# Row sums of the head-mixing softmax: added up by VectorE in place of ScalarE's accumulator output

## The reference, cut to what matters

```
scores = jnp.einsum('bshd,bsgd->bshg', q, k) * inv_sqrt_dk   # 16 x 16 per token
attn = jax.nn.softmax(scores, axis=-1)
out = jnp.einsum('bshg,bsgd->bshd', attn, v)
```

## Time and profile before

| | |
|---|---|
| median of three runs | 6372.72 us |
| profiled execution | 6376.72 us, span 6374.9 us |
| TensorE (PE) busy | 5567.3 us, 87% |
| VectorE (DVE) busy | 4532.6 us, 71% |
| ScalarE (ACT) busy | 3991.2 us, 63% |
| GpSimd (POOL) busy | 1513.1 us, 24% |
| mean granted TensorE clock | 0.892 |

### The profile page before, as it was taken

One profiled execution on the slowest core, in us unless ns is written; L12 is line 12 of the kernel. 1 busy time (PEld: TensorE's weight loads), 2 busy tenths in 40 slices (PEclk: granted clock), 3 DMA queues, 4 the chain that ended last, 5 costly groups with the idle time before them and its releaser, 6 DMA issues. The chain is left out here.

```text
span 6374.9 us, 111016 instructions
## 1 busy us (share of the span) xinstructions
PE 5567.3 (87%) x38530; PEld 3816.5 (60%) x38530; DVE 4532.6 (71%) x16189; ACT 3991.2 (63%) x9761; POOL 1513.1 (24%) x2564
## 2 busy tenths in 40 slices
PE   5889889898988989889898988889899898989976
PEld 3566566566656666566566656656556566656643
DVE  1377777677786677786677787767687676786774
ACT  2566666666676666676665676766576665666642
POOL 0122222222222222222222222222222222222221
PEclk7789898999999899898998989989898999988865
DMA  2000000000000000000000000000000000000000
GB/s 83 4 4 8 4 10 6 6 6 6 8 6 10 4 8 6 6 8 6 6 8 5 8 6 10 6 6 6 6 8 6 6 8 5 7 6 8 3 4 6
DMA packets 29382, 53.45 MB, mean 8 GB/s; under 512 B 8145, under 2 KB 9810, under 8 KB 27986
## 3 DMA queue, kind: packets, MB, share of 16 engines
q1 hardware_dynamic: 28770, 45.73, 2.3%
HBM read 37.33 MB, written 8.39 MB: 7 GB/s over the span
## 5 line engine op out<-in xcount | busy, mean ns | idle before, releaser
L997 POOL TENSOR_TENSOR t_pr<-t_pr,sc 128x512 f32<-128x512 f32 x512 | 654.4, 1278 | 1298.2 <-ACT t_pr L921 1296.4
L970 DVE MATCH_REPLACE8 wk<-m,wk 128x256 f32<-128x256 f32 x2048 | 822.9, 410 | 0.0
L966 DVE MAX8 m<-wk 128x8 f32<-128x256 f32 x2048 | 759.6, 413 | 0.0
L407 DVE TENSOR_REDUCE m_nm<-bankM 128x2 f32<-128x512 f32 x1024 | 651.1, 682 | 74.2 <-PE bankM L397 73.2
L732 ACT ACTIVATE xk_area<-bankH,xb 64x256 f32<-64x256 f32 x1024 | 479.8, 469 | 343.9 <-PE bankH L638 325.8
L456 PE MATMUL bankM<-m_q,m_kT 32*128 32x512 f32 x2048 | 652.2, 720 | 0.0
L927 ACT ACTIVATE t_pr<-t_pr,t_nm 128x256 f32<-128x256 f32 x1024 | 463.6, 502 | 196.0 <-POOL t_pr L997 192.3
L397 PE MATMUL bankM<-m_kT,m_q 32*128 32x256 f32 x4096 | 537.5, 389 | 24.8 <-DVE m_nm L407 15.7
L797 DVE TENSOR_REDUCE xnm<-bankH 128x4 f32<-128x512 f32 x256 | 176.1, 688 | 467.6 <-PE bankH L661 467.2
L498 PE MATMUL bankT<-ident,t_pr 128*128 128x128 f32 x2048 | 380.7, 316 | 140.6 <-ACT t_pr L927 139.6
L991 POOL TENSOR_SCALAR mx<-m 128x2 f32<-128x2 f32 x512 | 118.0, 231 | 1584.9 <-DVE wk L970 1579.8
(11 more groups left out here) (208 smaller groups left out, 11837.7 us busy)
## 6 DMA issues: line engine op xcount, KB each, us to landing
xin<-x_in SPq DMA_DIRECT2D x32, 256.0 KB, 3.1
ctxA<-ctx_in SPq DMA_DIRECT2D x32, 256.0 KB, 2.6
ctxB<-ctx_in SPq DMA_DIRECT2D x32, 256.0 KB, 2.8
out<-x SPq DMA_DIRECT2D x32, 256.0 KB, 2.2
w<-w_w SPq DMA_DIRECT2D x2, 1024.0 KB
xwq<-w_xwq SPq DMA_DIRECT2D x1, 1024.0 KB
xwk<-w_xwk SPq DMA_DIRECT2D x1, 1024.0 KB
xwv<-w_xwv SPq DMA_DIRECT2D x1, 1024.0 KB
```

What stands on the lines that cost most here:

```text
L407: nc.vector.tensor_reduce(b["nm"][:, i % 2, 2 * (i // 2) + x, :], banks[u % 4][:].rearrange("p (j s) -> p j s", j=2), AX.X, ALU.max, negat ...
L966: link.inc(nc.vector.max(top, src[:, t, :]))
L970: m = nc.vector.match_replace(out=wk[:, k, t, :], in_to_replace=take, in_values=src[:, t, :], imm_value=-BIG)
L997: nc.gpsimd.tensor_tensor(sp_[:, u % 2], taken[:, u % 2], sc[:, u % 3], ALU.mult).then_inc(g["sp_mul"], 1)
```

## The change

The exponentials lose `accum_out`. VectorE gets one `tensor_reduce` for each quad that adds up the rows of the four tiles in `xp`, and signals a new semaphore `hm_rs`, for which the reciprocal behind it waits. Nothing else of the program differs.

```
@@ COUNTS
-              ... hm_rr=8, hm_s=8, ...
+              ... hm_rr=8, hm_rs=8, hm_s=8, ...
@@ scalar_h
                         nc.scalar.activation(xp[s % 3][:, i, :], bankH[0][:, i * P:(i + 1) * P], ACT.Exp,
-                                             bias=xnm[:, c:c + 1], accum_out=xrs[:, c:c + 1]).then_inc(g["hm_ex"], 1)
+                                             bias=xnm[:, c:c + 1]).then_inc(g["hm_ex"], 1)
@@ vector_h
                     dve.wait_ge(*at(g["hm_ex"], 4 * q + 4))
+                    nc.vector.tensor_reduce(xrs[:, 4 * q:4 * q + 4], xp[q % 3], AX.X, ALU.add).then_inc(g["hm_rs"], 1)
+                    dve.wait_ge(*at(g["hm_rs"], q + 1))
                     nc.vector.reciprocal(xrr[:, 4 * q:4 * q + 4], xrs[:, 4 * q:4 * q + 4]).then_inc(g["hm_rr"], 1)
```

More of the change, by code:

```diff
@@ L101 @@
               crs_qT=2, crs_rd=2, crs_s=16, crs_sp=4, crs_st=16, crs_v=1, crs_va=1, crs_x=1, crs_y=1, ctxA_in=16, ctxB_in=16, dveC=1,
-              dveH=2, dveT=240, hm_ev=48, hm_ex=32, hm_nm=8, hm_o=8, hm_ot=8, hm_pn=8, hm_proj=12, hm_pt=8, hm_rr=8, hm_s=8, hm_tr=8,
+              dveH=2, dveT=240, hm_ev=48, hm_ex=32, hm_nm=8, hm_o=8, hm_ot=8, hm_pn=8, hm_proj=12, hm_pt=8, hm_rr=8, hm_rs=8, hm_s=8, hm_tr=8,
               hm_vev=4, hm_vtr=4, hm_x2=1, hm_xb=1, hm_y=1, latT=1, lat_ps=1, len_in=16, lin_o=1, lin_xb=1, lin_y=1, ln0_rstd=1, ln0_stat=5,
```

## The result

The changed kernel takes 6497.5 us (median of 4 runs) beside 6380.7 us of the kernel before: ratio 1.0182, 95% interval 1.0152 to 1.0211. It is slower, by 116 us where 88 were forecast (6497.5 us where the forecast has 6460). The profiled executions lie 6491.8 and 6376.7 us, 115 us apart, with a mean granted clock of 0.881 and 0.892.

A forecast was written before the change was run, and what follows sets the result against it. VectorE was taken to bound the full stretches, where it never pauses; 89 us there plus 10 in open stretches less 11 from dropped reads gave +88 us, forecast 6460 us, 8-in-10 range 6390 to 6540.

The forecast's parts named there:

- The full stretches, 124 x 0.72 = 89: Where VectorE never pauses, each of 124 quads' reduction and wait adds its full 0.72 us: 89 us.
- in the full stretch TensorE is not what is awaited, so I cost it at nothing: GpSimd normalising 0.72 us later per quad was priced at zero, since TensorE is not awaited in stretches where VectorE never pauses.
- At most 22 us come back from the reads, I take 11: Dropped ScalarE reads gain only in open stretches, where scores wait for exponentials: at most 62 x 4 x 0.09, half taken.
- The open stretches let a tenth through, 10: Where VectorE has idle time, its waits absorb most of 132 x 0.72 = 95 us of additions; 10 us remain.
- the 2 to 3 expected: Sign in the open stretch: VectorE's wait at line 797 should shrink by 2 to 3 us.
- The sum: Whole kernel: 89 + 10 - 11 = +88 us on the profiled 6376.7 us; forecast 6460 us, 1.4% slower.
- The top of the forecast's own range, 6505: Upper end of the forecast's own range, 6420 to 6505, from path terms up to 89 + 30 and a 30 us clock shift.
- TensorE is the true bound, the additions are absorbed: Rival: in the full stretches VectorE's additions fill slack and only the excess counts, about 6385 us; chance 0.17.
- ScalarE's gain decides: Rival: in the open stretch dropped reads outweigh the additions, faster, about 6281 us if all reads count; chance 0.05.
- Every reduction counts: Rival: open-stretch quads delay the next maximum too, so all additions cost, 6373 + 184 - 11 = 6546 us; chance 0.10.
- The reduction is stretched by GpSimd's traffic: Rival: GpSimd's traffic slows VectorE's sum to, say, twice its length, giving 6548 us; chance 0.03.
- If the mean granted clock moves by more than 0.01, part of the difference is the clock's: Sign: a shift of TensorE's mean granted clock above 0.01 means part of the difference is not the order's.

The follow-up runs named there:

- e4: The change for quads 5 to 8 of each sample alone, quads 1 to 4 keeping the accumulator output; 1.0200 of the kernel before, 127 us slower.
- e3: The change for quads 1 to 4 of each sample alone, quads 5 to 8 keeping the accumulator output; 1.0039 of the kernel before, 25 us slower.
- e5: The changed kernel with each reduction made twice, the first into an unread spare tile; 1.0442 of the kernel before, 281 us slower.
- e2: The kernel before with accumulator reads kept and VectorE's sums added into a spare tile, with the reciprocal's wait; 1.0163, 103 us slower.
- e1: The kernel before without the accumulator reads, no reduction added, reciprocals reading a constant 8; 0.9924, 48 us faster.
- e6: The kernel before with reads kept and VectorE's sums added into a spare tile, without semaphore or reciprocal's wait; 1.0337, 214 us slower.
- e10: e6's kernel unchanged, repeated on another occasion; 1.0271 of the kernel before, 173 us slower.
- e8: The kernel before with filler matmuls ahead of each key projection and the scores of quads 1 to 4; 0.9868, 84 us faster.
- e9: The changed kernel with the same filler matmuls as e8; 1.0053 of the kernel before.
- e11: The kernel before with more filler, 512 columns ahead of each query and key projection and all eight quads' scores; 0.9940, 38 us faster.

## Why the prediction was right, point by point

**That it is slower, and from where: right.** The full stretches carry the price (e4 against e3, and 4.0 us per sample in the traces), twice the reductions cost more than twice the time (e5), and the instruction costs what its neighbour's row said, 674 ns with a wait of 0.03 us ahead of the reciprocal.

**"The full stretches, 124 x 0.72 = 89": the place right, the size too small.** By the traces a full stretch grew by 4.0 us where the forecast has 2.9. The additions' own part, 2.3 us of busy time, was forecast well; the 1.75 us of new pauses was not forecast at all. The term that was mis-sized is "in the full stretch TensorE is not what is awaited, so I cost it at nothing". In the first pass the late reductions make the matmuls of line 397 wait for line 407 (15.7 to 52.8 us in the whole span), 13 us more of the stretch lie at half clock, and there TensorE is awaited, for 52.7 us more in total. The stretch grows by 6.5 us. In the second pass no half clock is added, nothing new is awaited, and the same additions cost 1.6 us, less than forecast. That e2 measures 103 us for the whole VectorE half, near the 99 of the sum, is luck: in its trace the full stretch is 5.9 us longer than before (164 us in 28 samples) and the open one 2.5 us shorter.

**"At most 22 us come back from the reads, I take 11": wrong size.** e1 gives 48 us (27 to 70). The forecast counted only the 62 times that the next scores wait for the exponentials. The trace has most of the gain in the open stretch, as forecast: 2.6 of the 3.4 us per sample. With it go 5.6 us less at half clock. How much of the 2.6 is the reads' own length and how much the clock was not separated.

**"The open stretches let a tenth through, 10": possibly too small, hidden by the reads.** e3 has both halves in the open quads, for which the forecast has 10 - 11 = -1, and measured +25 (8 to 43). If the reads' gain lies in the open stretches, as the forecast assumed, the reductions there cost up to 25 + 48 = 73 of their 95 us, not 10. Line 797's wait shrank by 1.6 us per sample, less than the 2 to 3 expected, which points the same way. But this is worked out by adding halves, and e2, with these reductions and the reads, has an open stretch 2.5 us shorter than before. What the reductions of the open stretch cost by themselves stays open.

**The sum.** It came near, 88 for 115, partly by luck: the mechanism that it names gives 64 of the 113 us of the full stretches, and what it lacks there is made up in part by the rest, which lost 25 us with less half clock. The halves measured apart do not add up (55 for 116). The quads do within their intervals (25 and 127 for 116). How far a comparison between occasions reaches is seen in e6 and e10: the same kernel stands 214 and 173 us over before. A sum of parts is a rough tool for this kernel. The top of the forecast's own range, 6505, is also less than its terms give (6373 + 119 + 30 = 6522).

**The rivals.** "TensorE is the true bound, the additions are absorbed" (6385) falls by e2 and e5, yet its premise came true for part of the stretch, at half clock and against its sign. "ScalarE's gain decides" falls: the gain is 48 us (27 to 70), larger than forecast and still less than the price. "Every reduction counts" (6546) falls for the change, by e3; the second set of e5 costs as much as it would have it, 163 us, but in the trace not in the open stretch. "The reduction is stretched by GpSimd's traffic" falls: the 256 lie between 665 and 684 ns.

**The signs named ahead.** "If the mean granted clock moves by more than 0.01, part of the difference is the clock's": it moved by 0.011, just past it. The sign was right and too coarse. The loop takes 3.9 us more per sample. Half clock takes 5.5 us more in the sum of the three stretches, but this is 13.1 us more in the first pass's full stretch, 2.0 more in the open one, and less in the second pass's full stretch and the rest. With fillers on both sides (e8 and e9) the sum does not rise at all (26.9 and 26.7 us) and the full stretch still grows by 4.0. The mean was the wrong gauge; the place of the half clock within the body was the right one.

**What stays open.** The pauses of VectorE and the half clock of TensorE come together in the first pass's full stretch; what the additions would cost there at full clock no run shows, beyond the second pass, where they cost 1.6 us. Whether the pause of TensorE ahead of a fall causes it. Why e2's order of waits leaves the open stretch at half clock for only 7.4 us and e6's for 19.7: the place of e6's excess is shown, its cause is not. And by what path the fillers help: the open stretch has less half clock with them, the steps between are not shown. All stretches come from one profiled execution of each kernel.

## What to carry to other kernels

Find the stretch in which the engine that receives the work never pauses, and price each added instruction by the distance from its neighbour's start to its own; here 2.9 us of such additions cost between 1.6 us in a stretch whose clock held and 6.5 us in one whose clock fell. Then ask what the delayed engine hands to TensorE: here more half clock came with small new waits of TensorE, and an engine that was "never awaited" became the bound for some microseconds. Read length and granted clock stretch by stretch and pass by pass, in more than one body, since a mean clock or a single stretch can mislead. Measure both halves of such a trade by themselves and together, and do not expect them to add up; and when TensorE shows half clock inside a loop's body, a cheap filler matmul ahead of the wait is worth one run, here 1.3% below the kernel before (e8), 0.6% with more of it (e11).

## What the runs showed of the hardware

The length of the same work moves with the clock. Two open stretches of the second pass, in one execution of the kernel before, hold the same 222 matmuls:

```profile
1437.96:1463.99 26.03, 22.59 (x222) 14.01 (x220) 24.65 (x97) 23.22 (x75) 8.12 (x13) 1.00 0.00 1
4475.74:4513.10 37.36, 35.65 (x222) 20.26 (x220) 24.95 (x98) 24.01 (x75) 8.16 (x13) 0.62 0.00 1
```

At 1.00 it lasts 26.0 us, at 0.62 (28.4 us of it at half clock) 37.4 us: some 0.4 us of length for each microsecond at half clock.

Removing work can cost time: e6 asks 31 us less of VectorE than e2 and takes 111 us more (70 on the other occasion), and adding work can save it: e8 adds 92 us of matmuls and takes 84 us less. In both, TensorE's busy time moves with the result and against the work.

An accumulator read on ScalarE shows 207 ns and holds the engine for 90: without its 1024 reads the busy time falls by 93 us, not 212.

A sum from SBUF and a maximum from PSUM of the same 128x512 cost VectorE nearly the same, 674 and 686 ns. The 58 and 120 cycles that the Trainium skill, "VectorE: DVE Perf Modes", section on the TRN2 errata, gives would be some 65 ns of difference (an estimate from that page's figures, at its 0.96 GHz); the rows have 12, and the measurement decides.
